# Placed inverse blocks, a leaky step in two parts, and a new order of steps in a four-layer graph kernel

## The reference, cut to what matters

```python
# layer 0 (layer 2 alike, with x @ W, a bias a_i + c_j, log(adj + 1e-9), and out + x at its end)
logits = einsum('bhqd,bhkd->bhqk', q, k) / sqrt(32) + log(clip(adj, 1e-8))[:, None]
attn = softmax(logits); out = einsum('bhqk,bhkd->bhqd', attn, v)
x = layer_norm(x + out @ Wo.T + bo, gamma, beta)
# layer 1 (layer 3 alike)
fp = x @ W.T + b
m = (fp @ qw + qb) + (fp @ kw + kb).T + (1 - adj) * -1e9
m = where(m >= 0, m, 0.01 * m)                  # the leaky step
x = softmax(m) @ fp + x
```

## Time and profile before

| what | value |
|---|---|
| median of 3 runs | 1825.92 us (1824.29 to 1826.78) |
| profiled execution | 1827.11 us, of which the span of its instructions is 1825.2 us |
| PE busy | 1786.8 us (98%), mean granted clock 0.989 |
| PEld / DVE / ACT / POOL busy | 1676.6 / 1496.7 / 1345.0 / 562.3 us |
| chain that ended last, by engine | PE 95%, DVE 3%, ACT 1%, issue 1% |

### The profile page before, as it was taken

The page is one execution under the profiler, slowest core; times in us unless marked ns, Lnnn a source line. Parts: engine busy times, 40 slices in busy tenths (PEclk is TensorE's granted clock), DMA queues, the critical chain, the costliest instruction groups (busy, mean ns, idle before and its releaser), DMA issues.

```text
span 1825.2 us, 69034 instructions
## 1 busy us (share of the span) xinstructions
PE 1786.8 (98%) x28449; PEld 1676.6 (92%) x28449; DVE 1496.7 (82%) x3359; ACT 1345.0 (74%) x3664; POOL 562.3 (31%) x667
## 2 busy tenths in 40 slices
PE   6999999999999999999999999999999999999996
PEld 6899999999999999999999999999999999999985
DVE  4678888888888888888888888888888888888885
ACT  3577787787787787787787787787787787787774
POOL 2232332332332332332332332332332332332321
PEclk7999999999999999999999999999999999999998
DMA  3111111111111111111111111111111111111100
GB/s 110 34 31 40 46 36 40 46 37 40 46 37 40 46 37 40 46 36 40 46 37 40 46 37 40 46 37 40 46 37 40 46 37 40 45 37 40 40 14 18
DMA packets 48260, 74.57 MB, mean 41 GB/s; under 512 B 5456, under 2 KB 21968, under 8 KB 47952
## 3 DMA queue, kind: packets, MB, share of 16 engines
q1 hardware_dynamic: 47376, 69.49, 12.1%
q10 hardware_dynamic: 576, 0.68, 0.1%
HBM read 53.37 MB, written 16.78 MB: 38 GB/s over the span
## 4 chain that ended last, share of the span: by engine, by line
PE 95%; DVE 3%; ACT 1%; issue 1%; POOL 0%; DVEq 0%; POOLq 0%; ACTq 0%
PE banks L877 17%; PE banks L942 15%; PE banks L879 15%; PE banks L878 15%; PE banks L986 7%; PE banks L1093 7%; PE banks L977 6%; PE banks L965 3%; PE banks L992 3%; PE banks L1081 2%; PE banks L1087 1%; PE banks L1053 1%; PE banks L1047 1%; PE banks L951 1%; PE banks L1031 0%
## 5 line engine op out<-in xcount | busy, mean ns | idle before, releaser
L478 POOL TENSOR_TENSOR weights_B<-weights_B,adj 128x512 f32<-128x512 f32 x64 | 82.4, 1288 | 815.9 <-ACT weights_B L551 815.9
L792 DVE TENSOR_TENSOR weights_A<-banks,adj 128x512 f32<-128x512 f32 x192 | 131.1, 684 | 77.2 <-ACT banks L547 77.1
L456 POOL TENSOR_TENSOR xt_lo<-x_t,xt_hi 128x512 fp32r<-128x512 f32 x64 | 82.1, 1282 | 335.6 <-ACT xt_hi L580 335.6
L877 PE MATMUL banks<-w_hi_f,xt_hi 128*128 128x258 f32 x512 | 164.6, 321 | 0.6 <-DVE xt_lo L656 0.6
L768 DVE TENSOR_REDUCE least_B<-banks 128x4 f32<-128x512 f32 x256 | 162.8, 678 | 0.0
L877 PE MATMUL banks<-w_hi_v,xt_hi 128*128 128x258 f32 (+1 forms) x512 | 152.2, 297 | 10.5 <-DVE w_lo_v L656 9.8
L768 DVE TENSOR_REDUCE least_cols_A<-banks 128x4 f32<-128x512 f32 x256 | 158.4, 681 | 4.5 <-PE banks L942 4.5
L636 ACT ACTIVATE logits<-logits,f_inv 128x128 f32<-128x128 f32 x256 | 90.9, 415 | 86.8 <-DVE f_inv L855 86.7
L877 PE MATMUL banks<-xt_hi,w_hi_q 128*128 128x256 f32 x512 | 150.5, 294 | 0.0
L879 PE MATMUL banks<-w_lo_v,xt_hi 128*128 128x258 f32 (+1 forms) x512 | 146.5, 286 | 0.0
L878 PE MATMUL banks<-w_hi_f,xt_lo 128*128 128x258 f32 x512 | 145.8, 285 | 0.0
(11 more groups left out here) (185 smaller groups left out, 6068.5 us busy)
## 6 DMA issues: line engine op xcount, KB each, us to landing
x_t<-x_t_dram SPq DMA_DIRECT2D x64, 256.0 KB, 2.7
x_in<-x_dram SPq DMA_DIRECT2D x64, 256.0 KB, 2.6
out_dram<-x_out SPq DMA_DIRECT2D x64, 256.0 KB, 2.0
adj_t<-adj_t_dram SPq DMA_DIRECT2D x64, 128.0 KB, 2.1
adj<-adj_dram SPq DMA_DIRECT2D x64, 128.0 KB, 2.6
scratch<-weights_dram SPq DMA_DIRECT2D x9, 256.0 KB, 6.6
scratch<-weights_dram ACTq DMA_DIRECT2D x2, 256.0 KB, 4.8
out_bias<-L_gnn_bo_dram ACTq DMA_DIRECT2D x1, 128.0 KB, 7.5
```

Of the source, the lines that this page charges most:

```text
L478: pool.tensor_tensor(units, units, weight_of[where][:, G.four, :, :].unsqueeze(2).broadcast_to([P, GROUP, 2, P]), ALU.mult).then_inc(first ...
L792: dve.tensor_tensor(weights[where][:, n, :].rearrange(units, g=GROUP, h=2), bank[SCORE_BANKS[n]].rearrange(units, g=GROUP, h=2), weight_of ...
L877: pe.matmul(out_ap, left_hi(k), right_hi(k), start=(k == 0), stop=False)
```

## The change

- **Inverses.** VectorE's third instruction of `den` writes to a new tile `inv_both`. A new GpSimd step `den` multiplies it by `own`, a 0/1 pattern that says which rows belong to which unit, and writes `inv_parts`, now 128 rows by 4 x 128 columns. `wide` of TensorE becomes one matmul of 512 columns with a single `spread` matrix, and waits for `inv_placed`, which GpSimd signals.
- **Leaky step.** `mask` of VectorE ends after L732's two instructions. A new ScalarE step `leak` writes 0.01 x of the logits to the PSUM bank that the mask used, and a new VectorE step `leak` takes the minimum of that and the logits, and then the reduction. The bank is free when that minimum is done.
- **Weighing.** GpSimd's `weigh` is gone; VectorE weighs all four quarters out of PSUM. ScalarE writes the first quarter to its bank like the others.
- **Order.** `ORDER` is new for all four engines; `FILLERS` is not.
- **Setup.** GpSimd builds the pattern for `own` and VectorE reduces it once.

```diff
-                        pool.wait_ge(adj0_ready if where == "A" else adj2_ready, G.no + 1)
-                        pool.wait_ge(exped[where], HALF * G.no + 1)
-                        units = weights[where][:, 0, :].rearrange("p (g h n) -> p g h n", g=GROUP, h=2)
-                        pool.tensor_tensor(units, units, weight_of[where][:, G.four, :, :].unsqueeze(2).broadcast_to(
-                            [P, GROUP, 2, P]), ALU.mult).then_inc(first_weighed[where], 1)
+                    elif name == "den":
...
+                        pool.wait_ge(inv_split[where], G.no + 1)
+                        pool.tensor_tensor(inv_parts[where][:, :, :],
+                                           inv_both[where][:, :].unsqueeze(1).broadcast_to([P, UNITS, P]),
+                                           own[:, :].unsqueeze(2).broadcast_to([P, UNITS, P]), ALU.mult
+                                           ).then_inc(inv_placed[where], 1)
...
+                    elif name == "leak":
+                        act.wait_ge(masked[where], GROUP * (G.no + 1))
+                        act.activation(bank[BANK["mask", where, 0]][:, 0:GROUP * P],
+                                       logits[where][:, :, :].rearrange("p g m -> p (g m)"), ACT.Copy, scale=SLOPE
+                                       ).then_inc(sloped[where], 1)
...
                 dve.wait_ge(masked[layer], GROUP * (G.no + 1))
-                dve.scalar_tensor_tensor(logits[layer][:, :, :], logits[layer][:, :, :], SLOPE,
-                                         logits[layer][:, :, :], ALU.mult, ALU.min).then_inc(leaked[layer], 1)
+                dve.wait_ge(sloped[layer], G.no + 1)
+                dve.tensor_tensor(flat, bank[BANK["mask", layer, 0]][:, 0:GROUP * P], flat, ALU.min
+                                  ).then_inc(leaked[layer], 1)
...
-                for u in range(UNITS):
-                    last = pe.matmul(to[:, cols(u)], spread[:, u, :, :].rearrange("p r d -> p (r d)"),
-                                     inv_parts[s][:, :], start=True, stop=True)
-                return last
+                return pe.matmul(to[:, :], spread[:, :, :].rearrange("p r d -> p (r d)"),
+                                 inv_parts[s][:, :, :].rearrange("p u n -> p (u n)"), start=True, stop=True)
```

More of the change, by code:

```diff
@@ L174, in build_kernel @@
         inv_hi = {s: sb(f"inv_hi_{s}", [P, P], F32R) for s in "AB"}
-        inv_parts = {s: sb(f"inv_parts_{s}", [P, P], F32R) for s in "AB"}
+        inv_both = {s: sb(f"inv_both_{s}", [P, P]) for s in "AB"}
+        inv_parts = {s: sb(f"inv_parts_{s}", [P, UNITS, P], F32R) for s in "AB"}
         ot_hi = sb("ot_hi", [P, GROUP, DIM], F32R)
@@ L203, in build_kernel @@
         sums = sb("sums", [P, UNITS, HEAD_DIM])
-        spread = sb("spread", [P, UNITS, HALF, HEAD_DIM], F32R)
+        spread = sb("spread", [P, HALF, HEAD_DIM], F32R)
+        own_all = sb("own_all", [P, UNITS, HALF, HEAD_DIM // UNITS])
+        own = sb("own", [P, UNITS])
         spread_raw = weights["B"][:, 0, :].rearrange("p (u r d) -> p u r d", u=UNITS, r=HALF)
@@ L328, in last_reader @@
             if name in ("scores", "again"):
-                return (maxed[where], HALF * (g + 1)) if name == "scores" else (weighed[where], (HALF - 1) * (g + 1))
+                return (maxed[where], HALF * (g + 1)) if name == "scores" else (weighed[where], HALF * (g + 1))
             if name == "turn_max":
@@ L863, in turn @@
                         mask(where, G, turn)
+                    elif name == "leak":
+                        leak(where, G)
                     elif name == "mix":
```

67 lines of the change are left out of this document (40 added, 27 removed), and 40 rows, old and new, of the table ORDER.

## The result

| what | before | changed |
|---|---|---|
| median, same chip (10 runs each) | 1825.96 us (1824.29 to 1827.40) | **1819.75 us** (1816.28 to 1821.51) |
| ratio, 95% interval | | 0.9965 [0.9956, 0.9975] |
| span of the profiled execution | 1825.2 us | 1819.7 us |
| mean granted clock of the span | 0.989 | 0.985 |

The kernel is faster, by 6 us where 21 were forecast. I start again with the page: busy times, granted clock in 40 slices, shares of the chain, and GpSimd's placing with its count, busy us, mean ns and idle time before.

The account below looks back on a forecast made before the run. TensorE was taken as the bound: a 27.38 us turn, with -0.42, -0.10, +0.05 and +0.1, becomes 27.0. Over 63 turns that is -24 us, plus 3 for filling and draining: span 1804, time 1805 us, range 1780 to 1835.

Parts of the forecast that it names:

- What bounds the kernel: Claim that TensorE, 98% busy, sets the full turn by the sum of its spacings, with VectorE second at 82%.
- The spread: On TensorE, one 512-column matmul replaces four of 128 columns for each stream: -0.42 us a turn, between 0 and -0.50.
- The new neighbours: TensorE's new order has 10 changes between kinds of work a turn, not 11: -0.10 us, from -0.4 to +0.4.
- The unseen direction: TensorE going straight from few rows to few columns (scores A to use B), absent from the earlier trace; costed within -0.10 us.
- Place (a): TensorE's fc of layer 1 waits for VectorE's turn_x, 6.04 against 6.00 us after scores A: +0.05 us a turn.
- (b): TensorE's spread of stream B, due at 6.87 us, waits for GpSimd's placing at 6.85: cover zero, +0.1 together with (c).
- (c): TensorE's next scores B wait for VectorE's last weighing of stream A, both at 11.2 us: cover zero, +0.1 together with (b).
- the slower rival: GpSimd's queue delays the spread of stream B by 0.7 us: turn 27.6 us, 1843 us in all, chance 0.15.
- the "against": Argument against the slower rival: where VectorE's adj_t meets GpSimd's placing, VectorE would be idle anyway, waiting for the spread.
- The sum: Whole span: -0.38 us over 63 turns, -24 us, plus +3 for filling and draining (from -3 to +10), giving 1804 us.
- a turn of 27.3: Lower end of the rival that the cover gives way: waits of 0.4 to 0.5 us, 1821 to 1830 us, chance 0.10.
- the dear case of the unseen changes of kind: On TensorE, each unseen change costs like the dear one: +0.4 us a turn, TensorE's own sum up to 27.3.

Follow-up runs that it names:

- b_pool2: b_pool with GpSimd's bias of layer 0 and adj_t moved behind the placing of stream A: 1802.94 us, ratio 0.9875, 26.92 us a turn.
- a_spread4: The changed kernel with the placing taken out and four 128-column matmuls for the spread again: 1835.27 us, ratio 1.0055, 27.40 us a turn.
- a_order: The changed kernel with inverses, leaky step and weighing as before, so the new order alone: 1833.34 us, ratio 1.0041, 27.37 us a turn.
- b_spread1: The kernel before with the placing and one-pass spread alone, in the old order: 1837.91 us, ratio 1.0070, 27.50 us a turn.
- b_late: b_spread1 with TensorE's spread of stream B one step later and VectorE's product behind one more weighing: 1835.72 us, ratio 1.0056, 27.45 us a turn.
- b_pool: b_late with GpSimd's weighing of stream A moved directly behind the placing of stream B: 1834.35 us, ratio 1.0046, 27.43 us a turn.

## Why the prediction went wrong

- **What bounds the kernel:** right. TensorE's sum is the turn, in the changed kernel and in b_pool2.
- **The spread:** right in kind, a little too large in size. Forecast 0.24 us for a matmul of 512 columns, 0.23 measured, 0.32 behind a change of kind (0.24 and 0.08 forecast). But the forecast took the first pass behind the four matmuls at 0.12, and it takes 0.16 to 0.18, before as now. By starts the two spreads took 0.39 + 0.48 us and now take 0.55, which is 0.32 less; the turn lost 0.38 against a_spread4 and 0.35 against a_order, forecast 0.42. In b_pool2 the gain is 27.37 - 26.92 = 0.45, with one spread moved as well.
- **The new neighbours:** forecast -0.10, measured about -0.18 by a_order, if the wait at fc is taken out. The unseen direction, scores A to use B, costs what scores A to v's passes cost, 1.10 us, and 0.18 more than scores again in the earlier trace rows with its 0.92. By the Trainium skill (TensorEngine Tiling (Array Packing), Key Properties) a change of tiling mode drains TensorE; the trace agrees, with those 0.18 us for rows to columns.
- **Place (a):** right place, mis-sized. turn_x ended 919.56 + 0.68 - 914.27 = 5.97 us after scores A began (forecast 6.04), but fc started 0.15 us behind it, where I had 0.05 for a handover, and TensorE was free earlier. The wait is 0.16 us, not 0.05. No row of the forecast had shown the handover of 0.05; here it is 0.15.
- **The turn of 27.0 was partly luck.** The forecast's terms were -0.42, -0.10, +0.05 and +0.10 for (b) and (c); a_order and the changed kernel show about -0.35, -0.18, +0.17 and nothing. Both sums are near -0.36.
- **Place (b):** in time. The placing took 1.04 us, not 1.27, and ended 0.42 us ahead of the spread (0.26 if fc had not been late). The feeder of the slower rival was there as told: VectorE's adj_t took 0.76 us, where 0.28 is usual, and ended 0.15 us behind GpSimd's placing (920.92 and 920.77). VectorE would have been idle there, so it cost nothing, as the "against" said.
- **Place (c):** VectorE's last weighing ends at 923.56 + 1.88 = 925.44; TensorE's last pass starts at 925.46 with the scores behind it, at 925.67. The cover was near zero and held.
- **VectorE's load:** 1565.4 us, 86% and not 91%. I had mixed two shares: 86% is that of the span, with fill and drain, and a full turn (914.27 to 941.29) has 24.24 us of it in 27.02, that is 90%, where I had 24.6 and 91%.
- **The sum, and here it failed:** "In filling and draining the chains are bare: [...] I take +3, from -3 to +10." It was **+15.5** (14.7 by the medians), outside the term's own range. The term counted added steps and not the order. A new order lays every chain of a turn out anew, and where not all streams run, gaps that another group's work filled stay open: the order alone brings 8.7 us by a_order. Part of that is TensorE's clock, which falls in the gaps: spare products give back 6.1 us in the new drain against 1.4 in the old. I had named the cold clock, but at the start alone, and for the end nothing. The smaller fault is 63 turns for 59 full ones, and 0.38 for 0.355: 0.355 x 59 is 20.9 us and not 24.
- **The chances:** the sign and the wide range (1780 to 1835) held, and so did the turn (26.8 to 27.2), but 1819.75 us lies above the forecast's own band, 1792 to 1818. What came was the last and least of the rivals, "the start or the end going otherwise by more than 10 us", at 0.03: it was 12.5 off. Two slips in the rivals changed nothing: a turn of 27.3 gives 1824 us by the forecast's sum, not 1821, and the dear case of the unseen changes of kind gives 27.4 and not 27.3. The slower rivals did not come. The late spread of the rival from GpSimd's queue, priced at 1843 us, is seen in b_spread1 (1838 us), but for another reason: not GpSimd's queue held it but VectorE's inverses, and the placing itself takes 1.04 us. The held VectorE addition is real too, and decides from b_late on. So the one-pass spread does hang on where GpSimd works, and the new order was one way to make that fit. It was not the only one: with the old order, a new one for GpSimd alone and one step moved on TensorE and on VectorE (b_pool2), the drain is 3.4 us longer than before and the fill 1.7 shorter, together +1.7 and near the forecast's +3, and the time is 1802.9, near its 1805. That kernel has neither the new weighing nor the new leaky step, so this doesn't confirm the forecast's term.

What stays open is how the 6.3 us of the fill divide between the parts of the change, and how much of the order's cost in the drain is the clock.

## What to carry to other kernels

Cost the fill and the drain of a pipelined kernel with as much care as its turn: when the order changes, every chain in them is a new one, and TensorE's clock can fall in the gaps it opens. Change one thing at a time where an order is involved: one gain (the spread) came in one edit with a part that only cost (the weighing) and one that gained nothing (the leaky step), and the gain is worth 23 us without them, once its own neighbours are placed (b_pool2). When a very short VectorE instruction on SBUF operands takes as long as a large GpSimd one and ends with it, move every GpSimd instruction from that spot, not just the one that stands there now.

## What the runs showed of the hardware

- **VectorE and GpSimd exclude each other over a tiny instruction.** An addition of 128 x 4 in SBUF takes 0.15 us alone, 0.55 beside a GpSimd instruction of 128 x 256 that ends with it, and 1.05 to 1.26 beside one of 128 x 512; VectorE's work out of PSUM on either side of it keeps its 0.68. By the Trainium skill (SBUF — State Buffer, Who interferes with whom) an instruction of VectorE with two SBUF inputs and one of GpSimd that reads SBUF exclude each other; the trace agrees, and shows what it can cost: 0.5 us a turn, 31 us from b_pool to b_pool2. Before the change the same addition was held for 0.55 us and TensorE didn't wait for it: the step to its mask was 0.12 us there too. A VectorE instruction of 128 x 256 with one SBUF input is held as well: adj_t, 0.28 us alone, has a median of 0.75 in the changed kernel, beside the placing.
- **GpSimd is faster when one operand stands still along the row.** The placing (L485, with `own` read as one value for each 128 columns) takes 1.04 us for 128 x 512, and so does `bias` of layer 3 (L458, with one column of `out_col` for 256). Repetition alone doesn't do it: the weighing (L486), which reads each adjacency tile twice, and `bias` of layer 0 (L452), which reads a row of 256 twice, take 1.28 to 1.30, like `turn_x` with two full operands (L464). In the kernels on the old order most placings of stream A take 1.42, which no run explains.
- **A fall of the clock in the drain** from the full level (granted 1.00) to the half (0.50) took a mix of eight matmuls from 1.09 to 2.05 us.
